# Segment ends and carries turned by 32x32 blocks on VectorE, bond scores behind the sums, and POOL's waits at gathers of their own

## The reference

```python
h = relu(layernorm(x))                                     # 12500 x 64
h_edge = ((h[src] + edge_attr_64) @ W).reshape(-1, 2, 64)  # 200000 edges
s = einsum('ehd,hd->eh', h_edge, attn_l) + einsum('nhd,hd->nh', (h @ W).reshape(-1, 2, 64), attn_r)[dst]
s = where(s > 0, s, 0.2 * s)
ex = exp(s - segment_max(s, dst)[dst])
ft = segment_sum(h_edge * (ex / segment_sum(ex, dst)[dst])[..., None], dst)
h = ft.mean(axis=1)                                        # mean over the heads
h = relu((h - h.mean(0)) / sqrt(h.var(0) + 1e-5) * gamma + beta)
return x + h
```

## Time and profile before

| what | value |
| --- | --- |
| time, median of 3 runs | 2634.44 us (2633.02 to 2635.84) |
| profiled execution, its own time | 2635.88 us |
| its span, first to last instruction | 2634.1 us |
| granted TensorE clock, mean | 0.646 of full speed |
| PE busy | 1146.7 us, 44% |
| PE weight loads | 770.4 us, 29% |
| VectorE busy | 1087.5 us, 41% |
| ScalarE busy | 120.4 us, 5% |
| POOL busy | 1482.3 us, 56% |
| mean DMA rate | 57 GB/s |

### The profile page before, as it was taken

The page is one execution under the profiler, slowest core; times in us unless marked ns, Lnnn a source line. Parts: engine busy times, 40 slices in busy tenths (PEclk is TensorE's granted clock), DMA queues, the critical chain, the costliest instruction groups (busy, mean ns, idle before and its releaser), DMA issues.

```text
span 2634.1 us, 23299 instructions
## 1 busy us (share of the span) xinstructions
PE 1146.7 (44%) x7218; PEld 770.4 (29%) x7218; DVE 1087.5 (41%) x3276; ACT 120.4 (5%) x243; POOL 1482.3 (56%) x1573
## 2 busy tenths in 40 slices
PE   1504544434534443553443345344335434534446
PEld 1402333223323322332332233233223223322325
DVE  5444444334334433433443343344344334434436
ACT  1310000000000000000000000000000000000001
POOL 7271456656655565665566566556656655665660
PEclk9956766666656665665666566666666666666656
DMA  5111212212211211221122122112212211221213
GB/s 161 59 27 56 66 44 71 47 44 50 69 46 45 71 47 44 52 66 47 45 71 48 43 58 61 47 45 71 48 43 67 52 46 46 71 48 43 71 31 101
DMA packets 72404, 149.42 MB, mean 57 GB/s; under 512 B 29854, under 2 KB 32712, under 8 KB 65752
## 3 DMA queue, kind: packets, MB, share of 16 engines
q0 software_dynamic: 50016, 52.85, 11.7%
q1 hardware_dynamic: 21146, 91.29, 9.8%
q10 hardware_dynamic: 1112, 3.73, 0.6%
HBM read 141.16 MB, written 6.60 MB: 56 GB/s over the span
## 4 chain that ended last, share of the span: by engine, by line
another core or an unknown queue 51%; DVE 33%; issue 9%; PE 3%; ACT 2%; DVEq 1%; DMA 0%; ACTq 0%
DVE acc L1309 5%; DVE work L998 4%; DVE ohT_i L1140 2%; DVE onehot L1134 2%; DVE scans L1225 1%; DVE scaled L1281 1%; DVE scans L1226 1%; DVE ends L1131 1%; DVE mx L1260 1%; DVE mx L1259 1%; DVE pen_first L1121 1%; DVE p_r L1224 1%; DVE zw L1186 1%; DVE sdif L1261 1%
## 5 line engine op out<-in xcount | busy, mean ns | idle before, releaser
L552 POOL DMA_INDIRECT work<-h_tab,srcI x1499 | 1419.2, 947 | 1067.2 <-PE p_m L882 468.7
L1237 DVE COPY rows<-p_r 1x192 f32<-1x192 f32 x49 | 16.9, 345 | 1163.1 <-remote 1162.1
L873 PE MATMUL p_r<-ones,cin 1*32 1x1 f32 x98 | 12.7, 196 | 862.1 <-DVEq L971 862.0
L898 PE MATMUL po<-scaled,work 128*65 128x64 f32 x3104 | 291.5, 281 | 68.2 <-issue 65.4
L797 PE MATMUL p_s<-work,wpair 128*32 128x256 f32 x784 | 286.1, 529 | 58.5 <-issue 56.3
L898 PEld LDWEIGHTS po<-scaled,work 128*65 128x65 f32 x3104 | 286.1, 197 | 85.9 <-issue 85.2
L873 PEld LDWEIGHTS p_r<-ones,cin 1*32 1x32 f32 x98 | 8.5, 134 | 905.2 <-DVEq L971 903.9
L1309 DVE TENSOR_TENSOR acc<-acc,po 65x64 f32 x776 | 168.6, 217 | 113.5 <-remote 86.0
L788 PE MATMUL pt<-ident,work 128*128 128x128 f32 x784 | 187.1, 383 | 39.0 <-issue 34.9
L797 PEld LDWEIGHTS p_s<-work,wpair 128*32 128x32 f32 x784 | 112.7, 150 | 204.9 <-issue 184.3
L814 PE MATMUL p_s<-ohT_i,er_st 128*32 128x256 f32 x392 | 122.0, 410 | 111.5 <-issue 111.1
(11 more groups left out here) (194 smaller groups left out, 1086.2 us busy)
## 6 DMA issues: line engine op xcount, KB each, us to landing
work<-in_ea_t SPq DMA_DIRECT2D x49, 1024.0 KB
ohT_i<-in_dst_n SPq DMA_DIRECT2D x49, 512.0 KB
work<-h_tab,srcI POOLq DMA_INDIRECT x1499
er_run<-er_tab SPq DMA_DIRECT2D x784, 0.2 KB
h_tab<-acc SPq DMA_DIRECT2D x1, 2887.5 KB
work<-in_x SPq DMA_DIRECT2D x1, 2800.0 KB
out<-work SPq DMA_DIRECT2D x5, 448.0 KB
acc<-in_x ACTq DMA_DIRECT2D x3, 672.0 KB
```

Of the source, the lines that this page charges most:

```text
L552: pool.indirect_dma_start(out=row, out_offset=None, in_=x if c < RAW else h_tab, in_offset=bass.IndirectOffsetOnAxis(ap=srcI[:, c, j, g:g ...
L898: m = mm(bank[0:F1, w0:w0 + H * WIN], edge[c % 2][:, j, g, :], scaled[:, j * CG + g, :, :].rearrange("p h w -> p (h w)"), start=(j == 0), ...
```

## The change

- `ends` gets six blocks of 32x32 of which only column 0 is filled: two columns from the scans, two (`LINKF`, `LINKB`) straight from the penalties, two (`CONNF`, `CONNB`) by one copy. One VectorE transpose by 32x32 blocks then gives `rows`, whose partition 0 holds what `row_ps` held. The carries `cin` and `cout` are rows of partition 0 in two blocks of `carry`, and a second block transpose gives `cc`. PE's products L863 and L873, two copies out of PSUM and four semaphores (`scans_ok`, `ends_turned`, `carry_ok`, `carry_turned`) go. `ends` and `carry` are cleared once at the start.
- On VectorE, `mx` (the maximum of the two scans) is made after the carries are turned, and `make_e(c + 1, 0)` after the difference.
- On PE, `bond_scores(c + 1)` moves from ahead of the carries to behind the sums and `turn(c + 1, 3)`; `own_turn(c + 1)` moves behind the wait for `open_exp`, its place in PSUM moves from bank `p_r` to `p_m`, and the last chunk's `z_block(NZ - 2)` is no longer made in two parts.
- In `make_near` the wait for `own_turned` comes ahead of the one for the targets and ahead of L1140.
- POOL's waits: `LEAD` is 6. From chunk 6 on the four waits stand one gather later each (gathers 1, 9, 17 and 25, counted from 0). Chunks 3 to 5 wait for steps of the chunks one and two before them at gathers 4, 12, 20 and 28. Chunk 1 waits for copies of the start's rounds at gathers 12, 20 and 26, and chunk 2 for steps of the raw chunks at 12, 18 and 28.

```diff
-LEAD = 4
+LEAD = 6
...
-        link = sb("link", [R2, 2])
         TAILC, HEADC, CONNF, LINKF, CONNB, LINKB = range(6)
         ends = sb("ends", [R2, 6, R2])
-        rows = sb("rows", [1, 6, R2])
+        rows = sb("rows", [R2, 6, R2])
         tail_in = sb("tail_in", [1, H, CG + 1])
         head_in = sb("head_in", [1, H, CG + 1])
-        cin = sb("cin", [1, H, CG])
-        cout = sb("cout", [1, H, CG])
-        cc = sb("cc", [R2, 2])
+        carry = sb("carry", [R2, 2, R2])
+        cin, cout = (carry[0:1, i, :].rearrange("p (h g) -> p h g", h=H) for i in range(2))
+        cc = sb("cc", [R2, 2, R2])
...
-        row_ps = p_r[0:1, GROUP:GROUP + 6 * R2].rearrange("p (i r) -> p i r", i=6)
-        cc_ps = p_r[0:R2, GROUP + 6 * R2:GROUP + 6 * R2 + 2]
-        own_ps = p_r[:, 512 - H * NB4:512].rearrange("p (h b) -> p h b", h=H)
+        own_ps = p_m[:, 336:336 + H * NB4].rearrange("p (h b) -> p h b", h=H)
...
+            def keep_step(c, at):
+                if c >= LEAD:
+                    keep_step_late(c, at)
+                elif c >= RAW + 1:
+                    if at == 4:
+                        pool.wait_ge(scores_ok, c - 2)
+                    elif at == 12:
+                        pool.wait_ge(p_turned, c - 2)
+                    elif at == 20:
+                        pool.wait_ge(scores_ok, c - 1)
+                    elif at == 28:
+                        pool.wait_ge(p_turned, c - 1)
+                elif c == RAW:
+                    if at == 12:
+                        pool.wait_ge(raw_centred, RAW)
+                    elif at == 18:
+                        pool.wait_ge(raw_root, RAW)
+                    elif at == 28:
+                        pool.wait_ge(e_ok, NQ * RAW)
+                elif c == RAW - 1:
+                    if at == 12:
+                        pool.wait_ge(hT_ok, len(HT) // 2)
+                    elif at == 20:
+                        pool.wait_ge(hT_ok, len(HT) - 4)
+                    elif at == 26:
+                        pool.wait_ge(hT_ok, len(HT) - 1)
+            def keep_step_late(c, at):
+                if at == 1:
+                    pool.wait_ge(p_turned, c - 1)
+                elif at == 9:
+                    pool.wait_ge(sums_made, 2 * (c - 1))
+                elif at == 17:
+                    pool.wait_ge(sums_added, 2 * (c - 1))
+                elif at == 25:
+                    pool.wait_ge(scores_ok, c)
             def gather(c, k):
                 q = c % 2
                 if c >= 2:
                     pool.wait_ge(e_ok, NQ * (c - 2) + k + 1)
-                if c >= LEAD:
-                    if k == 0:
-                        pool.wait_ge(p_turned, c - 1)
-                    elif k == 1:
-                        pool.wait_ge(sums_made, 2 * (c - 1))
-                    elif k == 2:
-                        pool.wait_ge(sums_added, 2 * (c - 1))
-                    else:
-                        pool.wait_ge(scores_ok, c)
-                for j, g in tiles_of(c, k):
+                for n, (j, g) in enumerate(tiles_of(c, k), EPP * GQ * k):
+                    keep_step(c, n)
...
-                pe.wait_ge(scans_ok, c + 1)
+                if RAW <= c + 1 < NCH:
+                    turn(c + 1, 1)
+                pe.wait_ge(open_exp, c + 1)
                 if c + 1 < NCH:
                     own_turn(c + 1)
-                mm(row_ps, ones[0:R2, 0:1], ends[:, :, :].rearrange("p i r -> p (i r)"), start=True, stop=True
-                   ).then_inc(ends_turned, 1)
-                if c == NCH - 1:
-                    z_block(NZ - 2, z_made, zT_ok, [0])
-                if RAW <= c + 1 < NCH:
-                    turn(c + 1, 1)
-                if c + 1 < NCH:
-                    bond_scores(c + 1)
-                pe.wait_ge(carry_ok, c + 1)
-                for i, t in enumerate((cin, cout)):
-                    m = mm(cc_ps[:, i:i + 1], t[:, :, :].rearrange("p h g -> p (h g)"), ones[0:1, 0:1],
-                           start=True, stop=True)
-                m.then_inc(carry_turned, 1)
-                pe.wait_ge(open_exp, c + 1)
                 mm(fb_ps, ones[0:1, 0:F1], fexp[:, :], start=True, stop=True).then_inc(open_all, 1)
...
                 if c + 1 < NCH:
+                    bond_scores(c + 1)
                     near_scores(c + 1)
...
+            step(v.memset(ends[:, :, :], 0.0))
+            step(v.memset(carry[:, :, :], 0.0))
...
-                also(v.tensor_scalar(link[:, 0:1], drow[:, GROUP:GROUP + 1], drow[:, 0:1], -BIG,
+                also(v.tensor_scalar(ends[:, LINKF, 0:1], drow[:, GROUP:GROUP + 1], drow[:, 0:1], -BIG,
-                step(v.tensor_scalar(link[:, 1:2], drow[:, 1:2], drow[:, GROUP + 1:GROUP + 2], -BIG,
+                step(v.tensor_scalar(ends[:, LINKB, 0:1], drow[:, 1:2], drow[:, GROUP + 1:GROUP + 2], -BIG,
                                      ALU.not_equal, ALU.mult))
...
-                for i, end in ((CONNF, pen[:, 0:1]), (LINKF, link[:, 0:1]), (CONNB, pen[:, GROUP:GROUP + 1]),
-                               (LINKB, link[:, 1:2])):
-                    (also if i != LINKB else step)(v.tensor_scalar(ends[:, i, :], ident[0:R2, 0:R2], end, None, ALU.mult))
+                step(v.tensor_copy(view(ends[:, CONNF, :], [[(CONNB - CONNF) * R2, 2], [1, 1]]), view(pen[:, :], [[GROUP, 2], [1, 1]])))
...
+                dve.wait_ge(own_turned, c + 1)
                 dve.wait_ge(near_in, 16 * (c + 1))
                 also(v.tensor_tensor(ohT, ohT_i[:, :, :], view(tgt[:, c * NB4:(c + 1) * NB4], [[1, NB4], [0, GROUP]]),
                                      ALU.is_equal))
-                dve.wait_ge(own_turned, c + 1)
...
-                v.tensor_tensor(ends[:, 0:2, :], view(ident[0:R2, :], [[0, 2], [1, R2]]),
-                                view(scans[:, :], [[1, 2], [0, R2]], GROUP - 1), ALU.mult).then_inc(scans_ok, 1)
-                step(v.tensor_tensor(mx[:, :], fw, bw, ALU.max))
-                if RAW <= c + 1 < NCH:
-                    make_e(c + 1, 0)
-                if last:
-                    z_stat(NZ - 5, zT_ok)
-                dve.wait_ge(ends_turned, c + 1)
-                step(v.tensor_copy(rows[:, :, :], row_ps))
+                step(v.tensor_copy(view(ends[:, TAILC, :], [[(HEADC - TAILC) * R2, 2], [1, 1]]),
+                                   view(scans[:, :], [[1, 2], [1, 1]], GROUP - 1)))
+                step(v.transpose(rows[:, :, :].rearrange("p i r -> p (i r)"), ends[:, :, :].rearrange("p i r -> p (i r)")))
                 def rw(i, hd):
-                    return rows[:, i, hd * CG:(hd + 1) * CG]
+                    return rows[0:1, i, hd * CG:(hd + 1) * CG]
                 for hd in range(H):
                     also(v.tensor_tensor_scan(tail_in[:, hd, 1:CG + 1], rw(LINKF, hd), rw(TAILC, hd),
@@ -1245,25 +1249,28 @@
                     (step if hd else also)(v.tensor_tensor_scan(view(head_in[:, hd, :], [[-1, CG]], CG - 1),
                                               view(rw(LINKB, hd), [[-1, CG]], CG - 1),
                                               view(rw(HEADC, hd), [[-1, CG]], CG - 1), -BIG, ALU.add, ALU.max))
-                also(v.tensor_tensor(cin[:, :, :], tail_in[:, :, 0:CG],
-                                     rows[:, CONNF, :].rearrange("p (h g) -> p h g", h=H), ALU.add))
-                step(v.tensor_tensor(cout[:, :, :], head_in[:, :, 1:CG + 1],
-                                     rows[:, CONNB, :].rearrange("p (h g) -> p h g", h=H), ALU.add))
-                signal(carry_ok)
+                also(v.tensor_tensor(cin, tail_in[:, :, 0:CG],
+                                     rows[0:1, CONNF, :].rearrange("p (h g) -> p h g", h=H), ALU.add))
+                step(v.tensor_tensor(cout, head_in[:, :, 1:CG + 1],
+                                     rows[0:1, CONNB, :].rearrange("p (h g) -> p h g", h=H), ALU.add))
                 step(v.tensor_tensor(fmax[:, :, :], cin[:, :, 0:1], head_in[:, :, 0:1], ALU.max))
                 step(v.tensor_tensor(fdif[:, :], cin[:, :, 0], fmax[:, :, 0], ALU.subtract))
                 signal(open_diff)
-                dve.wait_ge(carry_turned, c + 1)
-                step(v.tensor_copy(cc[:, :], cc_ps))
-                step(v.scalar_tensor_tensor(mx[:, :], pen_first[:, :], cc[:, 0:1], mx[:, :], ALU.add, ALU.max))
-                step(v.scalar_tensor_tensor(mx[:, :], pen_last[:, :], cc[:, 1:2], mx[:, :], ALU.add, ALU.max))
+                also(v.transpose(cc[:, :, :].rearrange("p i r -> p (i r)"), carry[:, :, :].rearrange("p i r -> p (i r)")))
+                step(v.tensor_tensor(mx[:, :], fw, bw, ALU.max))
+                step(v.scalar_tensor_tensor(mx[:, :], pen_first[:, :], cc[:, 0, 0:1], mx[:, :], ALU.add, ALU.max))
+                step(v.scalar_tensor_tensor(mx[:, :], pen_last[:, :], cc[:, 1, 0:1], mx[:, :], ALU.add, ALU.max))
                 v.tensor_tensor(sdif[:, :], sL, mx[:, :], ALU.subtract).then_inc(diff_ok, 1)
                 if last:
```

(38 more changed lines are left out.)

## The result

The changed kernel takes 2385.98 us in the median (2383.8 to 2394.7, 4 runs) against 2635.14 us; the ratio is 0.9062 (95% interval 0.9038 to 0.9085). The forecast was 2425 us, with a range of 2230 to 2530. The profiled execution takes 2383.8 us, 252 less than the one of before.

The account below looks back on a forecast made before the run. PE signals held until gather streams end, 1.41 us per gather, bound the kernel. From 2635.9 us, 50 (start) and 151 (42 periods, 51.1 to 47.5) gave 2435, median 2433; with 2400 for period 46.7, 2425 was taken, range 2230 to 2530.

Parts of the forecast that it names:

- The hold: PE signals stop some 7 us into a gather stream and come out at its end, 1.41 us per gather.
- step 1: Ends and carries turned on VectorE: 0.55 us for both transposes, new chain to the turned exponents 6.7 us.
- step 2: The hold moves from L1237 to L1281; the 4.43 us after it run inside it, gaining 4.4 us per chunk.
- step 3: Bond scores behind the sums: scores fall into the hold, stream cut at 16 gathers, period 47.5 us, bounds 45.3 and 49.
- the other order: Scores just pass and `p_turned` is held over 24 gathers: 46.7 us per chunk, 2400 us in all.
- the 201 of the sum: Total gain in us: 50 for the start and 151 for 42 periods, the last chunks +-3.
- step 4: POOL's waits one gather later, each alone: nothing, -0.6 to +0.6 us per chunk.
- step 5: Waits for chunks 1 to 5: h table 12 us earlier, chunk 6's gathers 50 us earlier, bounds 12 and 80.
- The hold did not go: Rival: waits in POOL's queue let PE's signals through and POOL binds, 2055 us; chance 12%.
- Bond scores do not starve: Rival denied here: PE gets instructions slowly behind the sums, 5 to 7 us more per chunk, 2845 us; chance 10%.
- the likeliest case: Main forecast, chance 74%: 2340 (period 45.3, start 50) to 2530 us (period 49.5, start 30).

Follow-up runs that it names:

- The turns alone: Changed kernel with POOL's old waits and the bond scores ahead of the exponents again: ratio 0.9322, 2417.8 us against 2592.6 for the kernel before.
- the four runs: One chip: changed kernel 2358.8 us; from it, bond scores back ahead of the exponents 2345.4, no early waits 2395.5, late waits at 0, 8, 16, 24 2380.9.

## Why the prediction was right

- *The bound.* The hold was read rightly, and the runs turn it into a rule for this kernel: `p_turned` comes 1.41 to 1.47 us times the number of gathers after the stream's start, for 12, 21 and 24 gathers, whenever PE's record ends. It is not as firm as its name: in the period shown the scores come 15 us into a stream (1241.04), 6.3 us after PE's record, and other signals follow one by one. The earlier trace rows had shown such a one at 161.93. That signals stop arriving some 7 us into a stream was too simple.
- *Ends and carries (step 1).* The two transposes take 0.37 and 0.23 us, 0.60 together where 0.55 was taken. From L1235 (1241.45) to the end of the exponents (1247.61) VectorE and ScalarE need 6.2 us, as worked out. PE's part behind it was taken for half a microsecond, as before; under the stream it takes 8.4 (to 1255.97). That did no harm only because the release comes later still.
- *What is late next (step 2).* The wait moved from L1237 to L1288 and ends with the stream. Forecast were 4.4 us per chunk. The turns alone have the forecast period, 46.67, but 175 us in 44 periods and the start together are less than 4.4 each; by the estimate above it is some 3.5 on that chip. This step is most of the gain (175 us of 232 to 249).
- *Bond scores (step 3).* Here the prediction chose wrongly. It took the scores to fall into the hold and to cut the stream at the 25th gather: 47.5 per period. They come at 1241.04, and gather 25 (counted from 0), which waits for them, goes at 1246.03 in an unbroken row of gathers: nothing is cut, and the period of 46.60 is that of the other order, for which the text had 46.7. Of the 51 us between the 201 of the sum and the 252 measured, 34 lie in the periods (185 instead of 151; this step and the next share them), 8 in the start and 9 in the last chunks, which had been left at nothing. The price of the move was wrong too: 0.8 per period was counted for it (47.5 for 46.7) and nothing ahead of chunk 6; on the changed kernel it costs 13 us, 9 of them ahead of chunk 6 and 0.06 per period. Alone it costs 28.
- *The waits' gathers (step 4).* Counted as nothing with ends of 0.6; on the changed kernel it is 0.74 per period and 22 us in all, since a second wait at one gather costs POOL 0.5 us. The possibility had been named and left at nothing. With it the other order gives 46.7 - 0.74 = 46.0, and the changed kernel has 45.85 on the chip of the four runs. In the first profile it has 46.60, because its first stream takes 12.1 us there in the median for 11.4; why is open. So that 46.60 lies so near 46.7 is in part luck.
- *The start (step 5).* The h table comes 20 us earlier (12 forecast). Chunk 6's point at the second gather comes 58 us earlier (50 forecast); its first gather, for which the text had 338, goes at 313.6, as it no longer waits. 50 us was right in size; the early waits bring 23 of them (37 us in all), as the table shows, and with the turns alone the point stands at 362.6 already, on another chip.
- *The rivals.* The hold did not go. Bond scores do not starve: their 16 products take 6.06 us (1226.57). But later in the stream PE's instructions do come slowly, 2.8 us apart at L889 and L892 (1250.16 to 1255.76), with no wait that the profile shows. It is not on the path, because these few end before the release; with 1255.97 against 1260.37 it is not far from it.
- *The range.* The upper end of the likeliest case is 2539 by its own terms (period 49.5, start 30), not 2530; nothing hangs on it. The forecast of 2425 missed by 39 us in all, and the misses of steps 3, 4 and 5 and of the last chunks all lay on one side.

The Trainium skill (SBUF — State Buffer, Who interferes with whom) would let the added VectorE copies delay gathers; by the one row with 0.1 us that had been 13 us. The mean gather went from 947 to 948 ns over 1499, 2 us in all: no run here shows more.

## What to carry to other kernels

When an engine waits for a signal of work that its record shows as long done, look for what ends the wait and count it: here each release of `p_turned` lay a fixed time per gather behind the start of a stream of indirect DMAs. Then take other engines' signals out of the stretch under the stream, by doing small transposes on the engine that needs them, rather than shorten work that nobody waits for. Break the stream at the signals on which the chain stands, each with a single wait, and measure each part of a bundle: one of the three parts here cost time.

## What the runs showed of the hardware

- PE's signals under a stream of indirect gathers come up to 26 us after their record, and the last of them at 1.41 to 1.47 us per gather from the stream's start (34.2 to 34.5 us for 24 gathers, 30.0 to 30.3 for 21, 17.5 to 17.8 for 12, 40 chunks each), although the gathers' rows lie 1.248 us apart. Earlier ones can pass: the scores come 5.7 to 15.7 us into the stream. What holds them (the semaphores' way, PE's instruction supply, or the gathers' descriptors) no run separates.
- A gather with two waits starts 0.71 us after VectorE goes on by the same signal, with one wait 0.23 us.
- A VectorE transpose by 32x32 blocks takes 0.37 us for 32x192 and 0.23 us for 32x64, against 0.16 us for a copy of two columns.
- PE's instructions under a stream can come slowly: the products of L889 and L892 start 2.8 us apart, with no releaser in the profile.
